# Rounding of the even blocks shared between VectorE and GpSimd in an attention kernel on one core

## What is computed

```
query = hidden_states @ Wq
hs = _mha(query, enc @ Wk, enc @ Wv)                 # 124 keys
ca_q1 = jnp.einsum('btc,th->bch', ca, Wq_ca)         # 384 rows of queries
ca_q1 = ca_q1[:, indices, :]                         # repeated over the 2048 rows
ca_hs1 = _mha(ca_q1, residual, residual)             # attention over all 2048 tokens
ca_q2 = ca_hs1 @ Wq
ca_hs2 = _mha(ca_q2, ca @ Wk_ca, ca @ Wv_ca)         # 4 keys
out = (hs + ca_hs2) @ Wout + b_out + residual
```

## Time and profile before

| | |
|---|---|
| median of 3 runs | 782.83 us (780.24 to 784.38) |
| the profiled execution's own time | 779.47 us |
| its span, first to last instruction | 777.7 us |
| mean granted TensorE clock | 0.991 of full speed |
| PE busy | 754.7 us (97%) |
| DVE busy | 538.2 us (69%) |
| ACT busy | 375.7 us (48%) |
| POOL busy | 171.8 us (22%) |
| attention over all tokens | about 205 to 284 us and about 564 to 643 us of the span |

### The profile page before, as it was taken

The page is one execution under the profiler, slowest core; times in us unless marked ns, Lnnn a source line. Parts: engine busy times, 40 slices in busy tenths (PEclk is TensorE's granted clock), DMA queues, the critical chain, the costliest instruction groups (busy, mean ns, idle before and its releaser), DMA issues.

```text
span 777.7 us, 13016 instructions
## 1 busy us (share of the span) xinstructions
PE 754.7 (97%) x4969; PEld 706.1 (91%) x4969; DVE 538.2 (69%) x910; ACT 375.7 (48%) x938; POOL 171.8 (22%) x232
## 2 busy tenths in 40 slices
PE   7999999999899999999999999999899999999998
PEld 5979999999688879999999999999878888999997
DVE  3456887888899985345546887888799995544442
ACT  1634445445588963223234445445479892222220
POOL 7025832111200001432220522111110001112130
PEclk9999999999899999999999999999989999999999
DMA  9424433443210025644434333444220002354431
GB/s 294 121 91 132 93 89 89 99 107 104 75 52 1 1 71 157 219 149 159 158 91 85 89 90 89 99 107 104 89 82 1 1 1 99 122 184 156 149 116 64
DMA packets 112821, 79.32 MB, mean 102 GB/s; under 512 B 91756, under 2 KB 93292, under 8 KB 112760
## 3 DMA queue, kind: packets, MB, share of 16 engines
q1 hardware_dynamic: 112760, 78.50, 34.4%
HBM read 48.56 MB, written 29.88 MB: 101 GB/s over the span
## 4 chain that ended last, share of the span: by engine, by line
PE 92%; DVE 4%; issue 2%; ACT 1%; DMA 0%; SPq 0%; DVEq 0%
PE PS L1138 30%; PE PS L1335 18%; PE PS L1321 8%; PE PS L1206 6%; PE PS L1112 6%; PE PS L1237 6%; PE PS L1228 5%; PE PS L1270 4%; PE PS L1084 2%; PE PS L1044 2%; PE PS L1303 1%; DVE e_hi L916 1%; PE PS L1254 1%; PE PS L1095 1%; PE PS L1159 1%
## 5 line engine op out<-in xcount | busy, mean ns | idle before, releaser
L1138 PE MATMUL PS<-mm_hi,xT_hi 128*128 128x280 f32 (+3 forms) x480 | 159.3, 332 | 0.0
L829 DVE TENSOR_REDUCE mpart<-PS 128x4 f32<-128x512 f32 x192 | 131.9, 687 | 39.5 <-PE PS L1112 39.2
L1138 PE MATMUL PS<-mm_lo,xT_hi 128*128 128x280 f32 (+3 forms) x480 | 157.5, 328 | 0.0
L1138 PE MATMUL PS<-mm_hi,xT_lo 128*128 128x280 f32 (+3 forms) x480 | 157.4, 328 | 0.0
L502 POOL TENSOR_TENSOR ex<-ex,rinv 128x992 f32<-128x992 f32 x32 | 59.1, 1846 | 223.2 <-DVE rinv L823 223.2
L613 ACT ACTIVATE ex<-PS,neg 128x124 f32<-128x124 f32 x256 | 90.0, 364 | 7.3 <-DVE gs L811 7.2
L1138 PEld LDWEIGHTS PS<-mm_hi,xT_hi 128*128 128x128 f32 x480 | 90.5, 189 | 0.8 <-issue 0.5
L1138 PEld LDWEIGHTS PS<-mm_hi,xT_lo 128*128 128x128 f32 x480 | 90.4, 188 | 0.4
L1138 PEld LDWEIGHTS PS<-mm_lo,xT_hi 128*128 128x128 f32 x480 | 90.3, 188 | 0.2
L924 DVE TENSOR_TENSOR e_lo<-e,e_hi 128x1536 fp32r<-128x1536 f32 (+1 forms) x46 | 77.3, 1688 | 4.8 <-ACT e_hi L664 4.0
L1112 PE MATMUL PS<-gT,aTm 128*128 128x256 f32 x384 | 76.6, 281 | 0.7 <-DVE mpart L829 0.7
(11 more groups left out here) (146 smaller groups left out, 1452.4 us busy)
## 6 DMA issues: line engine op xcount, KB each, us to landing
ex_kept<-ex SPq DMA_DIRECT2D x32, 512.0 KB, 2.9
ex<-ex_kept SPq DMA_DIRECT2D x32, 512.0 KB, 3.9
xin<-in_x SPq DMA_DIRECT2D x128, 80.0 KB, 2.9
xin<-in_x SPq DMA_DIRECT2D x32, 320.0 KB, 3.2
out<-res SPq DMA_DIRECT2D x32, 320.0 KB, 2.3
raw_kept<-raw SPq DMA_DIRECT2D x5, 512.0 KB, 2.6
mm_lo<-raw_kept SPq DMA_DIRECT2D x10, 186.0 KB, 3.9
wq_in<-in_L_xattn_Wq SPq DMA_DIRECT2D x2, 800.0 KB, 9.1
```

The source lines that it names most:

```text
L829: nc.vector.tensor_reduce(mpart[:, n // 2, :, 2 * (n % 2):2 * (n % 2) + 2, i].rearrange("p s k -> p k s"), PS[:, 6 + N % 2, :].rearrange(" ...
L1138: last = mul(PS[:, slot(T, k), p0:p0 + w], l[:, i % 2, j, :], rr[:, m0:m0 + w], start=(j == 0 and n == 0), stop=(n == 2), skip_group_check ...
```

## The change

For even blocks the rounding copy is shared. DVE copies columns 0 to 767 (the first two heads). GpSimd makes columns 768 to 1535 (the last two) by multiplying them with a broadcast one, the same form of instruction as line 534, and counts it in a new semaphore, `ehp_made`. DVE makes the low part of an even block in two halves, and waits for `ehp_made` before the second. PE waits for `ehd_made` and `ehp_made` before the matmuls with an even block's `e_hi`. Odd blocks stay as they were.

```
@@ gpsimd, behind the clearing of vcab
+                for p in range(0, QUADS, 2):
+                    N = b * QUADS + p
+                    pool.wait_ge(e_made, N + 1)
+                    if p >= HI_BUFS:
+                        pool.wait_ge(pv_done, N - HI_BUFS + 1)
+                    nc.gpsimd.tensor_tensor(e_hi[:, p % HI_BUFS, EW // 2:EW], e_of(p)[:, EW // 2:EW], ones([P, EW // 2], 0), ALU.mult)\
+                        .then_inc(ehp_made, 1)
@@ vector
-                        nc.vector.tensor_copy(e_hi[:, p % HI_BUFS, :], e_of(p)).then_inc(ehd_made, 1)
+                        nc.vector.tensor_copy(e_hi[:, p % HI_BUFS, 0:EW // 2], e_of(p)[:, 0:EW // 2]).then_inc(ehd_made, 1)
...
-                    cols = (0, EW // 2, EW) if p + 1 == QUADS else (0, EW)
+                    cols = (0, EW // 2, EW) if p + 1 == QUADS or p % 2 == 0 else (0, EW)
                     for c0, c1 in zip(cols, cols[1:]):
+                        if p % 2 == 0 and c0:
+                            dve.wait_ge(ehp_made, b * QUADS // 2 + p // 2 + 1)
                         nc.vector.tensor_tensor(e_lo[:, p % LO_BUFS, c0:c1], e_of(p)[:, c0:c1], e_hi[:, p % HI_BUFS, c0:c1].bitcast(F32), ALU.subtract)\
                             .then_inc(elo_made if c1 == EW else ehalf_made, 1)
@@ tensor, pv(p)
                     if p % 2 == 0:
                         pe.wait_ge(ehd_made, b * QUADS // 2 + p // 2 + 1)
+                        pe.wait_ge(ehp_made, b * QUADS // 2 + p // 2 + 1)
...
                     if p + 1 == QUADS:
-                        pe.wait_ge(ehalf_made, b + 1)
+                        pe.wait_ge(ehalf_made, (b + 1) * (QUADS // 2 + 1))
```

More of the change, by code:

```diff
@@ L330, in build @@
                                                                 sem("elo_made"), sem("pv_done"))
+        ehp_made = sem("ehp_made")
         acc_done, ehalf_made = sem("acc_done"), sem("ehalf_made")
```

## The result

| | before | changed |
|---|---|---|
| median | 781.54 us (4 runs) | 803.45 us (802.96 to 806.23, 4 runs) |
| the profiled execution's span | 777.7 us | 804.5 us |
| ratio | | 1.029, 95% interval 1.024 to 1.034 |

The changed kernel is slower by 22 us, against a forecast of 29 (812, range 800 to 826). With a run more, the median of before has moved from 782.83 to 781.54. The two profiled executions are not the median ones: that of the changed kernel is the slowest of its four (806.23 us), that of before is 2.1 us under its median. So their spans differ by 26.8 us where the medians differ by 21.9.

What follows compares the result with a forecast made beforehand. PE and DVE were taken as level in the attention over all tokens. DVE's pair was to grow from 4.62 to 5.54 us (4.16 + 1.35 + 0.03), 0.92 x 32 = 29.4 us, giving 812 us; range 800 to 826.

Steps and rivals of the forecast that it cites:

- What bounds the kernel: Attention over all tokens: PE about 4.4 us and DVE 4.42 us per even-odd block pair are level; DVE has nothing to give.
- The exclusion: Same stage: GpSimd's multiply and DVE's copies or differences wait for each other's whole instruction, so GpSimd's 1.47 us add to DVE.
- The price of the exclusion: Added to DVE's pair: 1.47 us less 0.12 us of hidden start-up, 1.35 us; bounds 1.23 and 1.77 us.
- DVE's own work: DVE's pair without GpSimd: 0.58 + 0.95 + 0.95 + 1.68 = 4.16 us, the even difference's halves costing 0.95 us each.
- The halved copy: DVE's rounding copy of even blocks: 768 columns take 0.55 us in place of 0.95, saving 0.40 us a pair.
- The sum: DVE's pair 4.16 + 1.35 = 5.51 us, 5.54 with `take(0)`, against 4.62: 0.92 x 32 = 29.4 us slower.
- my lower bound of 5.25: DVE's pair at best: 0.58 + 0.88 + 0.88 + 1.68 + 1.23 us; 21 us slower, 801 to 804.
- What else moves: Other engines in the stage: GpSimd's half is normally made during the block before, so PE's `ehp_made` wait costs nothing.
- The low clock: Rival, whole stage: PE's gaps lower its clock; 105 us more throughout, or 26 us in a quarter of pairs, 838; 5%.
- The rival with GpSimd too late: Even blocks: DVE keeps GpSimd out until it waits for `ehp_made`; 43 us slower, 822 or 826; 11%.

Runs made afterwards that it cites:

- run 3: The kernel before, plus an unneeded GpSimd multiply of 768 columns for every even block, from a constant table into a dead buffer: 812.68 us, ratio 1.040.
- run 7: The changed kernel, but GpSimd makes all 1536 columns of an even block and DVE copies nothing there: 838.78 us, ratio 1.074.
- Run 4: The kernel before, plus two GpSimd clearings of a dead buffer of 768 columns for every even block: 784.93 us, ratio 1.006.
- run 5: The changed kernel, but the low part of an even block in one piece, after DVE's wait for `ehp_made`: 804.0 us, ratio 1.029.
- run 9: The kernel before, with the low part of every block in halves and PE starting on the first half: 778.7 us, ratio 0.997.
- 6: The changed kernel, but GpSimd makes only 384 columns of an even block, DVE the rest: 793.12 us, ratio 1.015.
- 8: The changed kernel, but DVE copies all of block 0 in each batch, without GpSimd: 803.14 us, ratio 1.028.

## Why the prediction was right

**What bounds the kernel.** Right. PE and DVE are level in the stage, and what was added to DVE's pair was added to the kernel: 24.3 of 26.8 us lie there.

**The exclusion.** Right, and the term that carries the result. It was read from two differences of line 788 and one copy; runs 3 and 7 show it in the stage itself, in both directions: a copy held for 1.28 us, a multiply held for 1.6 us. Run 4 shows its limit: a clearing holds copies only, and little.

**The price of the exclusion.** Forecast 1.35 us a pair with bounds of 1.23 and 1.77, measured 1.28 (1.83 - 0.55, and again 2.23 - 0.95). GpSimd's 1.47 us for 768 columns were right to 0.01 (1.46 us in run 5, with DVE idle beside it). The estimate of 1.69 us by the Trainium skill's figure (GPSIMD Engine Reference, section "Elementwise — side-by-side cycle accounting") was too high for this form, in which the second operand is one broadcast element. What is hidden is 0.18 to 0.19 us, not 0.12: part of the start of GpSimd's operation is hidden too, most of what my lower bound allowed.

**DVE's own work.** This is the mis-sized term. I had put the two halves of the even difference at 0.95 + 0.95 us because each waits for a semaphore. In the trace they take 236.24 - 234.50 = 1.74 us together, 0.16 us a pair less. My 1.76 for the whole one was no fit measure either: it comes from a place where the odd difference started only as the even one ended. Where nothing is late the whole one takes 1.67 us (run 5). So a cut costs 0.07 us; I had charged 0.14. The halved copy was right: 0.55 us forecast and measured.

**The sum.** 5.51 became 0.58 + 1.74 + 1.67 + 1.28 = 5.27, next to my lower bound of 5.25. Over the 14 pairs from the second even copy to the last, slow ones included, the mean is 5.36 us (75.05 us; 215.94 to 290.99) against 4.62 before, 0.74 more instead of 0.92. Two times 14 pairs give 20.8 us, and the ends of the two stages 3.5. The two terms made the forecast 0.24 us a pair too long. The slow second pair and the pairs around `take(0)`, which I had not forecast in this size, gave back 0.06, so the 29.4 us are only 5.1 above the 24.3 of the profiled stages. Of the 8.8 us between 812.2 and 803.45, these are 5.1; 1.3 come from a median of before that was a little high, and 2.4 from the profiled executions, whose stages differ by more than the medians do. So the mechanism was forecast, and the errors of size lie nearly all on one side: the result is inside the range, at its lower end.

**What else moves.** PE's wait for `ehp_made` was hidden, except in block 0 of each batch, where PE stood 1.06 us for it. I had not named that. The low clock at the start of the stage, which I had only as a rival for the whole stage, took part in a small way: 0.8 to 0.9 us a batch. The rival with GpSimd too late did not come: only behind `take(0)` did the copy go ahead of a standing GpSimd, once in each batch, and in the next pair the order was back.

## What to carry to other kernels

An engine that the profile shows idle is not free for every kind of work: before moving work to GpSimd, look in the trace for a place where it already meets the same form of instruction on VectorE, and compare both durations with the undisturbed ones. If they stretch, add GpSimd's time to VectorE's, and compare the price of a column on either side (here 1.68 ns against 0.525). If a producer and a consumer are level, handing over in halves is worth a try before moving work: here a cut cost the producer 0.07 us, let PE start earlier, and won 0.3% in all (run 9), where moving work lost 2.9%.

## What the hardware showed that I had not expected

A cut is cheap. A single DVE difference of 768 columns shows 0.96 us, so two should take 1.92; in a row they take 1.74 from start to start, with a semaphore wait between them, against 1.67 for one of 1536 columns (run 5).

Which engine is held is not settled by who asked first: GpSimd's multiply, standing since 258.59, did not get in ahead of the copy at 259.48, but got in ahead of the steady pairs' copies, as of that at 237.91, which came 0.80 us after it. It is no accident of one pair. In runs 3, 5, 6 and 8 too the copy behind `take(0)` is not held, while a multiply stands since before it. In run 5 that multiply had stood for 0.81 us, as long as in the steady pairs of the changed kernel, so the time of standing does not decide:

```profile
259.90 2.69 POOL L550 TENSOR_TENSOR e_hi<-e,one 128x768 fp32r<-128x768 f32 x1 [3.45 <-ACT e L666]
260.71 0.55 DVE L924 CAST e_hi<-e 128x768 fp32r<-128x768 f32 x1
```

What decides was not tried. All these places have `take(0)` ahead of the difference under which GpSimd came to stand.
